# Up-sampled image: the leaky relu in ScalarE's scaling pass instead of a VectorE pass of its own, engine loops written out

## The reference

```python
x = x + _L0_conv_ref(_gn(x), ...)     # A = Wa x + ba; maps = softmax(Wb x); vecs = softmax(Wv x); Z = (A maps^T) vecs
x = x + _L1_conv_ref(_gn(x), bias, up_filter, down_filter)
# inside _L1_conv_ref, per channel image of 128 x 128:
y = _upfirdn2d_sep(x, up_filter, UP, 1, PADDING, float(UP * UP))   # -> 266 x 266
y = y + bias[None, :, None, None]
y = jnp.where(y >= 0, y, y * SLOPE) * GAIN                          # SLOPE 0.2, GAIN sqrt(2)
y = jnp.clip(y, -CLAMP, CLAMP)                                      # CLAMP 256
y = _upfirdn2d_sep(y, down_filter, 1, DOWN, (0, 0, 0, 0), 1.0)      # -> 128 x 128
```

## Time and profile before

| | us |
|---|---|
| median of 3 runs | 15492.39 |
| lowest and highest | 15478.86, 15493.5 |
| profiled execution, first to last instruction | 15490.4 |
| PE busy (matmuls) | 14319.3 |
| DVE busy | 12597.6 |
| ACT busy | 11639.9 |
| POOL busy | 10946.1 |

### The profile page before, as it was taken

One profiled execution on the slowest core, in us unless ns is written; L12 is line 12 of the kernel. 1 busy time (PEld: TensorE's weight loads), 2 busy tenths in 40 slices (PEclk: granted clock), 3 DMA queues, 4 the chain that ended last, 5 costly groups with the idle time before them and its releaser, 6 DMA issues.

```text
span 15490.4 us, 506727 instructions
## 1 busy us (share of the span) xinstructions
PE 14319.3 (92%) x158688; PEld 12344.3 (80%) x158688; DVE 12597.6 (81%) x28093; ACT 11639.9 (75%) x20736; POOL 10946.1 (71%) x16821
## 2 busy tenths in 40 slices
PE   7999999999999999999999999999999999999999
PEld 6788777887778877788777887777887778877788
DVE  7888878888888888888888887888878888788887
ACT  6777777777777777777777777777777777777777
POOL 5677766777667776677766777667776667766677
PEclk9999999999999999999999999999999999999999
DMA  3233222332223322233322333223332223322232
GB/s 86 69 92 99 72 67 69 90 99 74 69 69 86 99 77 69 69 84 99 81 69 69 81 99 84 68 69 80 97 87 69 69 77 96 89 69 70 74 97 53
DMA packets 1998134, 1233.83 MB, mean 80 GB/s; under 512 B 79748, under 2 KB 1931140, under 8 KB 1996804
## 3 DMA queue, kind: packets, MB, share of 16 engines
q1 hardware_dynamic: 1996804, 1217.21, 30.1%
HBM read 570.85 MB, written 268.44 MB: 54 GB/s over the span
## 4 chain that ended last, share of the span: by engine, by line
PE 51%; DVE 23%; issue 13%; ACT 6%; DMA 3%; DVEq 2%; POOL 0%; SPq 0%; ACTq 0%; POOLq 0%
PE ps L1158 51%; DVE nblk L873 4%; DVE z L1055 3%; DVE t L1049 3%; ACT yb L699 3%; DVE nrun L877 2%; DMA p<-t 2%; ACT z L682 2%; DVE mrun L862 2%; DVE srun L861 1%; DVE yb L1100 1%; DVE sth L985 1%; DVE stc L765 1%; DVE bexp L880 1%; DVE xh L1064 1%
## 5 line engine op out<-in xcount | busy, mean ns | idle before, releaser
L1158 PE MATMUL ps<-dn_t,yb 128*128 128x64 f32 (+1 forms) x32768 | 4328.4, 275 | 33.5 <-DVE z L1055 31.9
L1158 PEld LDWEIGHTS ps<-dn_t,yb 128*128 128x128 f32 x32768 | 3995.8, 192 | 84.2 <-DVE z L1055 54.2
L1100 DVE SCALAR_TENSOR_TENSOR yb<-yb 128x532 f32<-128x532 f32 x4096 | 3287.3, 803 | 758.6 <-ACT yb L699 737.1
L699 ACT ACTIVATE yb<-ps,bias_b 128x532 f32<-128x532 f32 x4096 | 2879.2, 704 | 892.0 <-PE ps L1158 786.1
L497 POOL TENSOR_SCALAR yb<-yb 128x532 f32<-128x532 f32 x4096 | 2701.9, 660 | 1101.6 <-DVE yb L1100 1094.4
L1158 PE MATMUL ps<-up,xn 128*128 128x266 f16 x12288 | 2047.5, 277 | 683.7 <-DVE t L1049 640.3
L667 ACT ACTIVATE t<-ps 128x266 f16<-128x266 f32 x4096 | 1578.4, 390 | 995.5 <-PE ps L1158 976.5
L1049 DVE TENSOR_TENSOR t<-ps,t 128x266 f16<-128x266 f32 x4096 | 1717.4, 423 | 616.4 <-ACT t L667 595.2
L1158 PE MATMUL ps<-up_a,t 128*128 128x138 f16 x15360 | 2030.7, 223 | 48.5 <-DMA t<-p 48.1
L1158 PE MATMUL ps<-up_b,t 128*128 128x138 f16 x15360 | 2026.4, 223 | 0.0
L489 POOL TENSOR_TENSOR xh<-xh,pt 128x512 f32 (+1 forms) x992 | 1632.8, 1647 | 473.2 <-DVE pt L908 473.1
(11 more groups left out here) (168 smaller groups left out, 30698.9 us busy)
## 6 DMA issues: line engine op xcount, KB each, us to landing
xc<-in_x SPq DMA_DIRECT2D x512, 512.0 KB, 3.8
xh<-in_x SPq DMA_DIRECT2D x480, 512.0 KB, 4.7
out<-xh SPq DMA_DIRECT2D x480, 512.0 KB, 3.2
p<-t SPq DMA_DIRECT2D x960, 128.0 KB, 2.4
t<-t SPq DMA_DIRECT2D x960, 128.0 KB, 2.4
t<-p SPq DMA_DIRECT2D x960, 128.0 KB, 2.4
xn<-in_x SPq DMA_DIRECT2D x64, 512.0 KB, 5.1
xh<-in_x SPq DMA_DIRECT2D x64, 256.0 KB, 3.1
```

Source lines behind the costliest of these rows:

```text
L699: act.activation(yb[:, i % YRING, :, :], y_ps[i % 2], ACT.Identity, scale=UPGAIN * GAIN, bias=bias_b[:, bass.ds(c0 + i, 1)]).then_inc(s_y, 1)
L1100: nc.vector.scalar_tensor_tensor(v, v, SLOPE, v, ALU.mult, ALU.max).then_inc(s_lr, 1)
L1158: return nc.tensor.matmul(o, l, r, start=start, stop=stop, skip_group_check=share)
```

## The change

In `filters` of ScalarE the two activations that write `yb` and `yr` change from `Identity` to `Prelu` with `alpha=SLOPE`. DVE's two leaky relu passes go, with the semaphores `s_lr` and `s_yl`; POOL's clip now waits for ACT's own semaphores `s_y` and `s_yr`. Besides, all `Fori` loops become Python loops, so that each engine has one straight list of instructions, and each `wait_alone` becomes a plain `wait_ge`, which the build attaches to the next instruction.

```diff
-        s_lr = sem("leaky_relu_done")
-        s_yl = sem("remainder_rows_leaky")
...
-        s_alone = sem("lone_waits")
...
-        def wait_alone(eng, semaphore, value):
-
-            eng.wait_ge(semaphore, value)
-            eng.sem_inc(s_alone, 1)
-
         def steps(eng, n, unroll, step, tail=1, head=0, ends=True):
...
-            with eng.Fori(1, n // unroll - tail) as k:
+            for k in range(1, n // unroll - tail):
                 for r in range(unroll):
                     step(unroll * k + r, r, lambda b: True, lambda a: True)
...
         def units(eng, attention, filters):
             attention(0)
-            with eng.Fori(0, UNITS - 1) as u:
+            for u in range(UNITS - 1):
                 filters(u, True)
                 attention(u + 1)
...
             def clip_image(g, i, par):
                 v = yb[:, i % YRING, :, :]
-                wait_alone(pool, s_lr, IMG * g + i + 1)
+                pool.wait_ge(s_y, IMG * g + i + 1 + YCREDIT)
                 nc.gpsimd.tensor_scalar(v, v, CLAMP, -CLAMP, ALU.min, ALU.max).then_inc(s_yc, 1)
...
             def remainder_high(g, par):
                 v = yr[:, par, :]
-                wait_alone(pool, s_yl, g + 1)
+                pool.wait_ge(s_yr, g + 1)
...
-                        act.activation(yb[:, i % YRING, :, :], y_ps[i % 2], ACT.Identity, scale=UPGAIN * GAIN,
+                        act.activation(yb[:, i % YRING, :, :], y_ps[i % 2], ACT.Prelu, scale=UPGAIN * GAIN, alpha=SLOPE,
                                        bias=bias_b[:, bass.ds(c0 + i, 1)]).then_inc(s_y, 1)
...
-                            act.activation(yr[:, par, :], o_ps[0:RR, 0:UP], ACT.Identity, scale=UPGAIN * GAIN,
+                            act.activation(yr[:, par, :], o_ps[0:RR, 0:UP], ACT.Prelu, scale=UPGAIN * GAIN, alpha=SLOPE,
                                            bias=bias_r[:, bass.ds((u % CPB) * NBAT + j, 1)]).then_inc(s_yr, 1)
...
                     dve.wait_ge(s_sq1, GROUPS * u + q + 1)
                     nc.vector.reciprocal(r1[:, 1:2], v1[:, 1:2]).then_inc(s_sm1, 1)
-                    wait_alone(dve, s_sm1, e + 4)
+                    dve.wait_ge(s_sm1, e + 4)
                     nc.vector.tensor_tensor(nmr1[:, 1:2], nm1[:, 1, 0:1], r1[:, 1:2], ALU.mult).then_inc(s_sm1, 1)
-                    wait_alone(dve, s_sm1, e + 5)
+                    dve.wait_ge(s_sm1, e + 5)
                     dve.sem_inc(s_r1, 1)
...
-                def remainder_leaky(g, par):
-                    dve.wait_ge(s_yr, g + 1)
-                    v = yr[:, par, :]
-                    nc.vector.scalar_tensor_tensor(v, v, SLOPE, v, ALU.mult, ALU.max).then_inc(s_yl, 1)
-
...
-                        if i == 1:
-                            remainder_leaky(g, par)
-                        v = yb[:, i % YRING, :, :]
-                        dve.wait_ge(s_y, IMG * g + i + 1 + YCREDIT)
-                        nc.vector.scalar_tensor_tensor(v, v, SLOPE, v, ALU.mult, ALU.max).then_inc(s_lr, 1)
```

More of the change, by code:

```diff
@@ L374, in swap_rows @@
                     if step:
-                        wait_alone(sp, s_swt[half], SWAP * n + 16 * step)
+                        sp.wait_ge(s_swt[half], SWAP * n + 16 * step)
                     sp.dma_start(to, source).then_inc(s_swt[half], 16)
@@ L411, in store_last @@
                     c, stored = last_half[half]
-                    wait_alone(sp, s_o, 2 * NBAT * (u + 1) - 1 + half + OCREDIT)
+                    sp.wait_ge(s_o, 2 * NBAT * (u + 1) - 1 + half + OCREDIT)
                     sp.dma_start(out_row[u, :, c, :], xh[:, c, :]).then_inc(stored, 16)
                 steps(sp, NBAT, 2, batch, 2)
-                wait_alone(sp, s_st[0], 16 * (NBAT // 2 * (u + 1)))
+                sp.wait_ge(s_st[0], 16 * (NBAT // 2 * (u + 1)))
                 if more:
@@ L420, in unit @@
                 store_last(1)
-                wait_alone(sp, s_st[1], 16 * (NBAT // 2 * (u + 1)))
+                sp.wait_ge(s_st[1], 16 * (NBAT // 2 * (u + 1)))
                 if more:
                     load_last(u + 1, 0)
-                wait_alone(sp, s_sl, 16 * (u + 1))
+                sp.wait_ge(s_sl, 16 * (u + 1))
                 if more:
                     load_last(u + 1, 1)
-            with sp.Fori(0, UNITS - 1) as u:
+            for u in range(UNITS - 1):
                 unit(u, True)
@@ L529, in norm_low_half @@
             def norm_low_half(g, par, h):
-                wait_alone(pool, s_xnh, 2 * g + h + 1)
-                wait_alone(pool, s_xs, 2 * g + h + 1)
+                pool.wait_ge(s_xnh, 2 * g + h + 1)
+                pool.wait_ge(s_xs, 2 * g + h + 1)
                 norm_low(par, 2 * h)
@@ L542, in first_batches @@
                 g = NBAT * u + 1
-                wait_alone(pool, s_r1, GROUPS * u + 1)
-                wait_alone(pool, s_xn, 2 * g)
+                pool.wait_ge(s_r1, GROUPS * u + 1)
+                pool.wait_ge(s_xn, 2 * g)
                 for h in range(2):
@@ L565, in clip_batch @@
                     if after(2) and i == (3 if before(1) else 6):
-                        wait_alone(pool, s_xnh, 2 * (g + 2) + 1)
-                        wait_alone(pool, s_xs, 2 * (g + 2) + 1)
+                        pool.wait_ge(s_xnh, 2 * (g + 2) + 1)
+                        pool.wait_ge(s_xs, 2 * (g + 2) + 1)
                         norm_low(par, 0)
@@ L575, in attention @@
                 for i in range(2):
-                    wait_alone(pool, s_xh[i], 16 * (NBAT // 2 - 1) * (u + 1))
-                wait_alone(pool, s_xa, 32 * (u + 1))
-                with pool.Fori(0, NBLK // 2) as k:
+                    pool.wait_ge(s_xh[i], 16 * (NBAT // 2 - 1) * (u + 1))
+                pool.wait_ge(s_xa, 32 * (u + 1))
+                for k in range(NBLK // 2):
                     gather_h(u, 2 * k, 0)
                     gather_h(u, 2 * k + 1, 1)
-                wait_alone(pool, s_xl, 16 * 3 * (u + 1))
+                pool.wait_ge(s_xl, 16 * 3 * (u + 1))
                 for par in range(2):
                     spread(u, par, par)
-                with pool.Fori(1, NBLK // 2) as k:
+                for k in range(1, NBLK // 2):
                     for par in range(2):
@@ L819, in _ @@
                 dve.wait_ge(s_xc[i], 16 * XCH // 2)
-            with dve.Fori(0, NBLK) as k:
+            for k in range(NBLK):
                 c_stats(k)
@@ L825, in link @@
                 ins.then_inc(s_small, 1)
-                wait_alone(dve, s_small, done)
+                dve.wait_ge(s_small, done)
             def norm0_stats(n, done):
```

50 lines of the change are left out of this document (25 added, 25 removed).

## The result

| | before | after |
|---|---|---|
| median of 4 runs each, us | 15487.88 | 15088.7 |
| lowest and highest | 15478.86, 15493.5 | 15080.81, 15107.49 |
| profiled execution | 15490.4 | 15087.6 |

The account below looks back on a forecast made before the run. PE plus its waits, chiefly for DVE's late `t1_low`, was taken as the filter-stage bound. Middle batches 11.8, start 1.5, outer batches 2.3 and swaps -1.5 gave 14.1 us per unit, 451 in all: 15040 us, range 14800 to 15330.

Parts of the forecast that it names:

- middle batches, and first and last two: Filter stage, per unit: 11.8 us from six plain and six group batches, 2.3 us from the first two and last two.
- start of filters: Start of each unit's filter stage: straight code removes PE's branch standstill and shortens chain links, 1.5 us per unit, bounds 0.5 to 2.0.
- swaps: Swap DMAs around batch 14: PE arrives earlier, waits longer and the clock may fall, -1.5 us per unit, bounds 0 to -3.5.
- attention: Attention stage: DVE-paced, no leaky relu, waits already attached, so 0; bounds 0 to 1.1 us per unit.
- The removed pass: DVE's leaky relu between ACT's `z` and PE's `up_rows`: per batch 0.70 us plain, 0.55 group, plus 0.26 at the clip.
- the clip: POOL's clip of image 0 at the batch's edge: starts sooner and isn't slowed without DVE's pass, 0.26 us.
- Group edge: Group batch's end: attached waits 0.12 plus loop and register steps 0.33, together 0.45 us on PE's path, bounds 0.12 to 0.58.
- the second rival: Small steps such as `nmr` get stuck beside POOL instructions, 5.7 us per unit back, time 15287; chance 0.20 (15180 to 15400).
- this chain hangs on loads and not on compute: Swap chain at batch 14, queued behind input loads: batch 13 gains nothing, and PE arriving earlier only waits longer.
- Prelu: ACT's existing 704 ns pass changes function at 0 added cost, bounds 0 to 704 ns; rival that Prelu is slower: 0.07.
- The two rows named for it: Profile rows supporting Prelu's zero added cost: an Identity over 532 elements at 704 ns, a Copy over 512 at 0.60 us.
- Contention: POOL's clip beside DVE's two-SBUF-input leaky relu: they exclude each other, clip 1.44 us; clips near 0.63 us expected after.

## Why the prediction was right, point by point

Per unit, in us, from the two lists of waits (differences divided by 32):

| step of the sum | predicted | measured |
|---|---|---|
| middle batches, and first and last two | 11.8 + 2.3 | 16.4 (`t1_low`, `z`, `xn`, `xb`: 786.5 to 262.8) |
| start of filters | 1.5 | -0.2 in waits ("issue" and `mvh`, 81.8, to `mvh`, 88.8) |
| swaps | -1.5 | -5.2 |
| attention | 0 | 0.9 (`tspr`, 29.0 to nothing) |
| PE's busy time | in the swaps' term | 0.8 |
| sum | 14.1 | 12.6, of 12.6 in the span |

The mechanism is the one predicted, but that the time came within 49 us is in part luck: more went beside DVE and POOL than was taken (2.3 us per unit), and attention and PE's busy time gave another 1.7; the swaps took 3.7 more than taken, and the start of filters gave 1.7 less in waits.

- **The removed pass.** Mechanism and places right: the idle at images 6 to 7 (0.69 and 0.55 us gone, 0.70 and 0.55 taken) and at the clip is gone. The clip was mis-sized: its place lost 0.46 us, not the 0.26 of idle that the view shows. The pair lost 1.99 us, predicted 1.96 (0.70 + 0.26 + 0.55 + 0.45), but the clip's 0.20 too little and some 0.15 of small places left out make up for the edge's 0.31 too much. The split between the two parts was wrong: the pass alone gives 1.82, not 1.51, the waits and loops alone 1.49, not 0.45. I took the register steps inside a batch for nothing, and I added two cuts of one queue as if each had its own idle time to end.
- **Group edge.** Mis-sized in the changed kernel: 0.14 us, not 0.45 (bounds 0.12 to 0.58). With the pass kept it is 0.47 (1.24 to 0.77), as worked out. With it out, `nmr` runs beside POOL's `xn`: 475 ns in the mean, against 193 with the pass kept and the loops out. That is the second rival, at a third of its price (0.49 us at the edge shown, not 1.11).
- **Start of filters.** Mis-sized. The standstill at the branch did go and the small product starts 1.0 us sooner after attention in the mean of 32 units (5.07 us behind `gaug`, 6.10 before). What I left out is that PE then waits 2.8 us for `mvh`, the 26 fillers run at the low clock for at least a part in 26 of the 32 units, and they end late: the first real matmul comes 10.43 us behind `gaug` in the mean, 11.06 before. Of the 1.5 us 0.6 are left.
- **Swaps.** Right in kind, at batch 14 (3.66 us), mis-sized in the whole: -5.2, beyond the bound of -3.5. The step that failed is "this chain hangs on loads and not on compute", applied to batch 14 only. The pass's removal costs 1.2 us per unit at the swaps (48.1 to 87.8), close to the 1.5 taken; the other 4 come with PE's straight list (4.1 in the run that changes it alone). In the middle batches the chain had a margin of 2.8 us; a faster PE left 1.7 of it, and the instruction fetches of PE's straight list used up the rest, which I had weighed as stops of PE and not as traffic.
- **Attention.** 0.9 inside the bounds of 0 to 1.1: it is `tspr` on POOL, whose loops went. With loops 29.8 us still stand in the run with the pass out alone; with the loops written out and the lone waits kept there are none.
- **Prelu.** 703 ns, as taken; without it the time is the same. The two rows named for it were weak support: 704 and 600 ns differ by 17%, their elements by 4%.
- **Contention.** The Trainium skill, page "SBUF — State Buffer", section "Who interferes with whom", says that a VectorE instruction with two SBUF inputs contends with a GpSimd instruction that reads SBUF. The mean clip fell from 660 to 630 ns, but it is 632 with the pass kept and the loops out, so that mean does not show the exclusion. POOL's busy time bears it out better: 10605.2 us with the pass kept, 9720.9 without it, both with the loops out; nearly all of that lies off the path.

## What to carry to other kernels

Two cuts in the queue of one engine are not to be added: each is worth the idle time that it ends alone, and together they end no more than the lateness there is. Read a place that comes once per unit in all units before multiplying it. Before counting gains of a faster stage, look at the serial DMA chain that runs beside it, its period and its margin; once it is late it issues behind the bulk loads and stays late, and small dependent DMAs belong on another queue than those. Attach the waits: with all lists straight that gave 152 us (15240.78 to 15088.7), while writing out the other engines' loops with their lone waits kept gave nothing (15215.14 and 15240.78). And weigh a list of 158688 matmuls before writing it out: a loop there, with its stop of some 2.7 us per unit, was 125 us faster than straight code.

## What the runs showed of the hardware that was not expected

- Straight code on PE fetched 1272 packets of 16 KB, 1.1 us each, 64 bytes per instruction; looped code 699, and next to none while two batches repeat. PE was not stopped by it; the swaps that met a packet took 2.83 instead of 2.45 us.
- The same DMA of a swap (128 KB) lands in 2.4 us alone, in 6.9 behind 1.5 MB in its queue.
- Behind an idle time of 2.78 us the granted clock was 0.50 for at least four us in one unit while PE was busy with fillers, and 26 of them took 5.92 us; in another unit, behind the same idle time, it was 1.00 and they took 3.11 us.
